# One-hots built by VectorE from broadcast rows of bin numbers, z from full-width operands, two banks for the partial sums

## The reference, cut to what matters

```
msg = silu(concat(h[src], h[dst], weight) @ mW1 + mb1)
msg = layer_norm(msg, ln_g, ln_b)
msg = silu(msg @ mW2 + mb2)
agg = segment_sum(msg, src, num_segments=6250)
```

## Time and profile before

| | |
|---|---|
| median of three runs | 2670.76 us |
| profiled execution, its time / its span | 2670.47 / 2668.8 us |
| sorting ends, first gather of `messages` | 599.5 us, 601.2 us |
| last sum of `messages` ends | 2149.9 us |
| PE / DVE / ACT / POOL busy over the whole span | 76% / 79% / 63% / 66% |
| PE / DVE / ACT / POOL busy from 700 to 1900 us | 1182 / 1119 / 1027 / 967 of 1200 us |
| granted TensorE clock from 700 to 1900 us | 1.00 (2.4 GHz) |
| DMA share and rate from 700 to 1900 us | 0.24, 72 GB/s |

### The profile page before, as it was taken

How to read it: one execution, slowest core, us unless ns; L and a number is a source line. 1 busy time by engine, 2 the same in 40 slices (tenths; PEclk the granted TensorE clock), 3 DMA queues, 4 the chain that set the end, 5 groups by cost and what they waited for, 6 DMA issues and landing times. The chain is left out here.

```text
span 2668.8 us, 63199 instructions
## 1 busy us (share of the span) xinstructions
PE 2025.3 (76%) x14160; PEld 1864.4 (70%) x14161; DVE 2099.3 (79%) x6765; ACT 1692.5 (63%) x3817; POOL 1770.6 (66%) x2247
## 2 busy tenths in 40 slices
PE   0000595008999999999999999999999969829980
PEld 0000584008999999999999999999999857719980
DVE  9994474028999999999999999999999837736666
ACT  5340121027888888888888888888888735418860
POOL 0007777737887878878878788788788715755660
PEclk9999997558999999999999999999999989959995
DMA  5000243012222222222222222222222354434548
GB/s 162 0 0 9 71 145 94 6 37 75 74 71 71 74 71 71 74 72 71 73 72 71 73 71 73 71 73 73 71 72 73 64 170 130 142 122 136 152 140 288
DMA packets 145565, 230.56 MB, mean 86 GB/s; under 512 B 33241, under 2 KB 101491, under 8 KB 145214
## 3 DMA queue, kind: packets, MB, share of 16 engines
q0 software_dynamic: 60672, 139.93, 18.0%
q1 hardware_dynamic: 75758, 81.69, 10.2%
q10 hardware_dynamic: 9040, 7.85, 0.9%
HBM read 167.41 MB, written 61.73 MB: 86 GB/s over the span
## 5 line engine op out<-in xcount | busy, mean ns | idle before, releaser
L1035 POOL DMA_INDIRECT rows<-b_rows,dst_row x838 | 841.8, 1004 | 229.7 <-issue 146.7
L1162 PE MATMUL ps_z<-w_hi,t_hi 128*128 128x256 f32 x1676 | 547.6, 327 | 0.0
L1163 PE MATMUL ps_z<-w_lo,t_hi 128*128 128x256 f32 x1676 | 468.5, 280 | 0.0
L1149 PE MATMUL ps_agg<-rows,onehot 128*126 128x256 f32 x1676 | 454.2, 393 | 18.8 <-DVE node_rows L1184 16.2
L1164 PE MATMUL ps_z<-w_hi,t_lo 128*128 128x256 f32 x1676 | 468.2, 279 | 0.0
L1068 ACT ACTIVATE rows<-rows,shift,rstd_m 128x256 f32<-128x256 f32 x838 | 452.5, 587 | 0.2 <-DVE shift L1192 0.2
L1184 DVE TENSOR_TENSOR node_rows<-node_rows,ps_agg 126x256 f32 x838 | 345.1, 412 | 105.6 <-issue 90.1
L460 POOL DMA_INDIRECT sorted_edges<-pay,place x245 | 242.7, 991 | 279.0 <-DVE place L802 199.4
L1095 ACT ACTIVATE rows<-rows 128x512 f32<-128x512 f32 x419 | 265.0, 632 | 187.9 <-DVE rows L1240 182.2
L1149 PEld LDWEIGHTS ps_agg<-rows,onehot 128*126 128x126 f32 x1676 | 281.3, 187 | 74.4 <-DVE node_rows L1184 23.1
L1045 POOL TENSOR_TENSOR rstd_m<-mv_m,half_m 128x2 f32<-128x2 f32 x419 | 306.3, 731 | 34.9
(11 more groups left out here) (316 smaller groups left out, 4360.3 us busy)
## 6 DMA issues: line engine op xcount, KB each, us to landing
x_e<-by_expert SPq DMA_DIRECT2D x56, 260.0 KB, 2.8
rows<-b_rows,dst_row POOLq DMA_INDIRECT x838
y_back<-y_rows SPq DMA_DIRECT2D x49, 252.0 KB
b_rows<-b_out SPq DMA_DIRECT2D x50, 126.0 KB
u_rows<-u_out SPq DMA_DIRECT2D x50, 126.0 KB
xh_rows<-xh_out SPq DMA_DIRECT2D x50, 126.0 KB
u_row_up<-u_rows SPq DMA_DIRECT2D x50, 126.0 KB
xh_row_up<-xh_rows SPq DMA_DIRECT2D x50, 126.0 KB
```

The source lines that it names most:

```text
L1035: nc.gpsimd.indirect_dma_start(rows[r][:, i, :], None, dram["b_rows"], bass.IndirectOffsetOnAxis(ap=dst_row[:, r, i:i + 1], axis=0)).then_ ...
L1149: mm = pe.matmul(ps_agg[0:BIN, i * D:(i + 1) * D], onehot[:, q, i, 0:BIN], rows[q][:, i, :], start=True, stop=True)
L1162: pe.matmul(z, t_hi[:, k, i, c, :], w2_hi[:, c, :], start=(c == 0), stop=False)
L1163: pe.matmul(z, t_hi[:, k, i, c, :], w2_lo[:, c, :], start=False, stop=False)
```

## The change

Three things are changed in `messages`, and a piece is added to `nodes_and_sort` that feeds the first:

1. The turned one-hots (bin number on the partition, edge along the free dimension) are no longer made on TensorE and copied by ACT. SP loads the row of bin numbers of four tiles into all 128 partitions (`rows_of`, 256 KB every second group) and the two weight words into partitions 126 and 127 of `onehot_t`; DVE compares the row with each partition's number in one `tensor_scalar`. SP's loads are issued two pairs of groups ahead. The small copy L1205 goes, and so do L1128 and L1082.
2. z is four plain float32 products a group instead of twelve float32r ones; the low half L1224 goes, and a `hold` on the statistics takes over its wait.
3. `ps_agg` becomes two banks in place of one, in the room of `ps_oh`; the sums wait for the group before the last instead of the last.

At the end of `nodes_and_sort`, GpSimd copies three of the four words of each edge apart, block by block through three buffers, and SP writes them to the new table `edge_words`.

```diff
+        def words_apart(b):
+            rows = (u_out, xh_out, b_out)[b % 3][:].rearrange("p i f -> p (i f)")[:, 0:(WORDS - 1) * P]
+            return rows.rearrange("p (w e) -> p w e", w=WORDS - 1)
...
             for b in range(BLOCKS):
-                sp.wait_ge(by_tile_in[b], 16)
+                n = min(P, TILES - b * P)
+                sp.wait_ge(words_ready, b + 1)
+                sp.dma_start(dram["edge_words"][:, b * P:b * P + n, :].rearrange("w t p -> t w p"),
+                             words_apart(b)[0:n]).then_inc(words_out[b % 3], 16)
+            for i in range(3):
+                sp.wait_ge(words_out[i], 16 * len(range(i, BLOCKS, 3)))
...
+            for b in range(BLOCKS):
+                n = min(P, TILES - b * P)
+                pool.wait_ge(by_tile_in[b], 16)
+                if b >= 3:
+                    pool.wait_ge(words_out[b % 3], 16 * (b // 3))
+                nc.gpsimd.tensor_copy(words_apart(b)[0:n],
+                                      by_tile[0:n, b, :].rearrange("t (p w) -> t w p", w=WORDS)[:, 1:, :]
+                                      ).then_inc(words_ready, 1)
...
+            def step(j, r, live):    # SP, in messages; AHEAD = 2
+                n = RING * j + r
+                if r % AHEAD or not live(0):
+                    return
+                q = r % (2 * AHEAD)
+                h, many = q // AHEAD, AHEAD if not isinstance(n, int) else min(AHEAD, GROUPS - n)
+                if live(2 * AHEAD):
+                    hold(sp, onehot_t_ready, n - 2 * AHEAD + many)
+                sp.dma_start(rows_of[:, q:q + many].rearrange("p g i e -> p (g i) e"),
+                             dram["edge_words"][0:1, ds(2 * n, 2 * many), :].broadcast_to([P, 2 * many, P])
+                             ).then_inc(rows_in[h], 16)
+                if live(2 * AHEAD):
+                    hold(sp, a_gathered, n - 2 * AHEAD + many)
+                sp.dma_start(onehot_t[BIN:P, q:q + many].rearrange("p g i e -> p (g i) e").bitcast(F32),
+                             dram["edge_words"][1:WORDS - 1, ds(2 * n, 2 * many), :]).then_inc(weights_in[h], 16)
...
-                    nc.vector.tensor_copy(onehot[:, r, :, BIN:P], tiles[:, :, 2:4]).then_inc(onehot_ready, 1)
+                    q = r % (2 * AHEAD)
+                    dve.wait_ge(rows_in[q // AHEAD], 16 * (2 * j + r // 4 + 1))
+                    if live(2 * AHEAD):
+                        dve.wait_ge(a_gathered, n - 2 * AHEAD + 1)
+                    nc.vector.tensor_scalar(onehot_t[0:BIN, q], rows_of[0:BIN, q], pcol[0:BIN, :], None, ALU.is_equal
+                                            ).then_inc(onehot_t_ready, 1)
...
-                    nc.vector.tensor_tensor(t_lo[:, k].rearrange("p i c e -> p (i c e)"), ps_rt[k][:],
-                                            t_hi[:, k].rearrange("p i c e -> p (i c e)").bitcast(F32),
-                                            ALU.subtract).then_inc(lo_ready, 1)
...
-                    if not live(5):
-                        dve.wait_ge(tile_stats, 2 * g + 2)
+                    hold(dve, tile_stats, 2 * g + 2)
...
-                    if live(6 + 1):
-                        pe.wait_ge(added, 2 * g + 1)
+                    pe.wait_ge(onehot_ready, g + 1)
+                    if live(6 + 2):
+                        pe.wait_ge(added, 2 * g - 1)
...
-                            pe.matmul(z, t_hi[:, k, i, c, :], w2_hi[:, c, :], start=(c == 0), stop=False)
-                            pe.matmul(z, t_hi[:, k, i, c, :], w2_lo[:, c, :], start=False, stop=False)
-                            mm = pe.matmul(z, t_lo[:, k, i, c, :], w2_hi[:, c, :], start=False, stop=(c == KC - 1))
+                            mm = pe.matmul(z, t_rows[:, k, i, c, :], w2[:, c, :], start=(c == 0), stop=(c == KC - 1))
```

More of the change, by code:

```diff
@@ L44 @@
 RING = 8
+AHEAD = RING // 4
 TABLE_P = P
@@ L330, in nodes_and_sort @@
         by_tile_turned = sem("by_tile_turned")
+        words_ready = sem("words_ready")
+        words_out = [sem(f"words_out{i}") for i in range(3)]
         slots_even = sem("slots_even")
@@ L483, in _ @@
                     packed[:, n * PACK:(n + 1) * PACK, :].rearrange("h e w -> h (e w)"), None).then_inc(scattered, 16)
+            for k in range(2):
+                pool.wait_ge(outs_stored[k], 16 * 3 * BINS // 2)
+            for b in range(BLOCKS):
[6 more added lines that the diff above has]
+                                      ).then_inc(words_ready, 1)
         @block.scalar
@@ L981, in messages @@
         onehot_ready = sem("onehot_ready")
-        onehot_turned = sem("onehot_turned")
+        rows_in = [sem(f"rows_in{h}") for h in range(2)]
+        weights_in = [sem(f"weights_in{h}") for h in range(2)]
         onehot_t_ready = sem("onehot_t_ready")
@@ L1017, in _ @@
             sp.wait_ge(table_in, 16)
+            def step(j, r, live):
[13 more added lines that the diff above has]
+                             dram["edge_words"][1:WORDS - 1, ds(2 * n, 2 * many), :]).then_inc(weights_in[h], 16)
+            pipeline(sp, step, 0)
         @block.gpsimd
@@ L1023, in _ @@
             nc.gpsimd.memset(half[:], -0.5).then_inc(start, 1)
-            pool.wait_ge(start, 1)
+            nc.gpsimd.iota(pcol[:], [[0, 1]], base=0, channel_multiplier=1, allow_small_or_imprecise_dtypes=True
+                           ).then_inc(start, 1)
+            pool.wait_ge(start, 2)
             def step(j, r, live):
@@ L1075, in step @@
                                          ).then_inc(msg_ready, 1)
[L1076 to L1083, removed]
                 if live(4):
@@ L1089, in step @@
                         act.wait_ge(z_ready, g - 1)
-                    nc.scalar.activation(t_hi[:, k].rearrange("p i c e -> p (i c e)"), ps_rt[k][:], ACT.Copy
-                                         ).then_inc(hi_ready, 1)
+                    nc.scalar.activation(t_rows[:, k].rearrange("p i c e -> p (i c e)"), ps_rt[k][:], ACT.Copy
+                                         ).then_inc(t_ready, 1)
                 if live(1):
@@ L1116, in step @@
                         pre = ps_pre[k][:, i * D:(i + 1) * D]
-                        pe.matmul(pre, onehot_t[:, k, i, :], a_hi[:, ds(b[i], 1), :].rearrange("p o f -> p (o f)"),
+                        pe.matmul(pre, onehot_t[:, q, i, :], a_hi[:, ds(b[i], 1), :].rearrange("p o f -> p (o f)"),
                                   start=True, stop=False)
-                        mm = pe.matmul(pre, onehot_t[:, k, i, :],
+                        mm = pe.matmul(pre, onehot_t[:, q, i, :],
                                        a_lo[:, ds(b[i], 1), :].rearrange("p o f -> p (o f)"), start=False, stop=True)
                     mm.then_inc(a_gathered, 1)
[L1122 to L1129, removed]
                 if live(4):
@@ L1172, in _ @@
             dve.wait_ge(table_in, 16)
+            dve.wait_ge(start, 2)
             def step(j, r, live):
@@ L1178, in add_sums @@
                 def add_sums(i, d):
-                    g = n - d
+                    g, k = n - d, (r - d) % 2
                     dve.wait_ge(part_ready, g + 1)
```

43 lines of the change are left out of this document (18 added, 25 removed).

## The result

The changed kernel takes 2680.36 us (median of 15 runs, 2675.63 to 2691.40) against 2670.76 (15 runs) for the kernel before on the same chip: ratio 1.0032, 95% interval 1.0022 to 1.0042. The forecast was 2682. The sum came out; its terms did not, and the experiments show which.

What follows compares the result with a forecast made beforehand. The prediction took POOL's own instructions, 3.567 us a group, to bound the loop. From the profiled execution: 2670.5 + 5 (once-only) - 6.3 + 12.6 (collisions) = 2681.8, say 2682 us; range 2650 to 2715, the forecast's own 2676 to 2700.

Steps and rivals of the forecast that it cites:

- POOL paces the kernel before at 3.567 us and keeps its pace: Loop: POOL runs its own instructions end to end at 3.567 us a group; disturbances add 0.080, 33.5 us over 419 groups.
- The prediction's own sign of being wrong: Changed loop: the forecast is wrong if L1042 waits for a releaser, or PE has no idle time while POOL has some.
- Once-only, +5: Outside the steady loop: sort's end +3.2 us (+1 to +8), loop's start +2 (0 to +4), sum +5.
- Collisions, -6.3 + 12.6: POOL meeting DVE in the loop: small collisions go, -6.3 us; in one group of eight POOL waits 0.24 longer, +12.6.
- rival B: Loop: shorter and longer collisions cancel, only the once-only 5 us are left, 2675.5 us; chance 0.25.
- z, +0.28 on PE: z's products on PE: twelve take 1.62 us before, four float32 products (eight passes) 1.90 after; 0.28 more work.
- PE's sum +0.03 and hidden: PE's group in the loop: +0.03 us (-0.15 to +0.35), hidden as long as it stays under POOL's.
- rival D: Loop: PE becomes the bound at 3.66 to 3.78 us against 3.647, +5 to +56 us, 2710 in the middle; chance 0.07.
- The banks, nothing won: Two banks for the sums: PE's 0.03 us idle time before L1149 goes, but PE is not the bound, so no gain.
- DVE's issue, 0.7 a group: Sign in the changed profile: DVE's idle time still in front of L1184 and larger, 0.7 us a group.
- DVE's step of 3.52: DVE's loop step, L1240 to L1240: 3.32 us without idle time becomes 3.52, still fitting under POOL's 3.567.
- SP's loads, nothing: SP's 256 KB load every second group: costed at nothing, issued over two groups ahead and hidden by the ring of four groups.

Runs made afterwards that it cites:

- without epsilon: The kernel before with POOL's addition of epsilon to the variance (L1042) left out: ratio 0.9745, 2607.2 us, 3.486 us a group.

## Why the prediction was right in sum, and where its steps failed

That 2682 met 2680 is in part luck: the once-only costs were 2 us too low, the loop's cost 5 us too high, and the two errors met in the sum. The mechanism that held is the one under the sum: POOL went on at its pace, and what was moved to DVE and PE did not lengthen the group.

- *POOL paces the kernel before at 3.567 us and keeps its pace.* Right: 0.25 us taken from POOL alone brings 2.6% there, and the loop holds 329 groups in 1200 us in both kernels. But in the changed kernel POOL no longer paces alone: the same 0.25 us brings 0.6%. The prediction's own sign of being wrong, PE without idle time while POOL has some, was all but seen: PE idles for 7 of 1200 us.
- *Once-only, +5.* The mis-sized term. Its two parts, +3.2 for the sort's end and +2 for the loop's start, measured +6.8 and +0.6. Of the 3.6 us that the sort's end took more, most lies in the rounds. From the first copy to the end of the last they took 10.15 us (593.52 to 603.67), where two rounds of 0.6 and 2.8 and a last copy make 7.4: a copy took 0.87 us, and the buffer of the first write was free 5.33 us after its issue (599.74 - 594.41), the second's 2.20 (602.82 - 600.62). What held the first write up, no row says. The rest, 0.8, lies behind the last copy, 4.33 us, where 2.8 for the write and the 0.7 that the kernel before takes from its last slots (599.49) to POOL's next instruction make 3.5.
- *Collisions, -6.3 + 12.6.* Here the step failed. By place in the loop's eight groups, leaving out the long pauses named at the end, the slow places have means of 3.73 and 3.74 us before and 3.70, 3.65 and 3.75 after; the eight together grew by 0.02, not by 0.24 at one place less 0.015 at each. The comparison cut to two columns gives 0.007 us a group, 3 us, and the intervals of the two times overlap. POOL's meetings with DVE move from one instruction to the other and largely cancel (in ns: L1086 +20, L1089 -10, each gather -3, POOL's idle time -6 a group). The Trainium skill ("SBUF — State Buffer", section "Who interferes with whom") gives the lock on the shared ports, and the rows agree that the engines hold each other up (194 against 206 ns above); that it lengthens a group by as much as I had, no run here shows. This is rival B's mechanism, with a larger once-only price.
- *z, +0.28 on PE.* +0.32: in steps without a wait the float32r products start 0.118 us apart, 12 x 0.118 = 1.41, and the float32 passes 0.216, 8 x 0.216 = 1.73. My two prices were both too high, by about as much. The 1.62 held 0.19 us of the last pass of the sums: z's first start is recorded 0.03 us behind that pass's and the next 0.306 later, and 0.03 + 0.306 is one pass and one product. The 0.24 held the gap behind the first pass of the sums (0.289 in the middle, before; the others are 0.216). The Trainium skill's four passes for true float32 ("FP8 and Floating Point Precision", section "TensorE Precision Notes") would make it, by estimate, 16 x 0.118 = 1.89; the trace has 1.73, so a float32 product costs 3.7 of the others here, still more than the three that it replaces.
- *PE's sum +0.03 and hidden.* The size failed, the hiding held by little: the middle values of the 26 starts of a step without epsilon, before, add up to 3.41 us, and the changed step takes 3.62, +0.21: z +0.32, L1128 -0.22, the gap before the sums and the last turn +0.12. That puts PE 0.05 above POOL's undisturbed pace and 0.03 below its mean, 3.65. So rival D was right that PE becomes a bound, beside POOL; its price (+5 to +56; the middle of it gives 2706, not 2710) was too high because I started from 3.63 for a PE that needs 3.41.
- *The banks, nothing won.* On the changed kernel, where PE is tight, they save 10 us; the kernel before was not run with two.
- *DVE's issue, 0.7 a group.* 0.48. The 0.23 + 0.2 of my own working had it; the 0.7 among the signs does not follow from them. DVE's step of 3.52 added the 0.2 and left out the 0.77 and the 0.41 of the same list; with them it is 3.16. The comparison took 0.374 for 0.41.
- *SP's loads, nothing.* DMA rose from 72 to 108 GB/s, and the loop did not.

## What to carry to other kernels

A busy share of 98.5% says little of an engine's own need: relieve the engine that sets the pace (here by leaving out one small instruction) and read the next bound, before spending one engine's room on another's. When a change leaves the time where it was, it may still have used up all of the slack: here the next good step, worth 2.6% on the old kernel, is worth 0.7% on the new one, other savings included. A stage that ends on GpSimd can cost more than its copies: here 1.6 us beyond its last write.

## What was not expected of the hardware

- Behind its last copy POOL needed 4.33 and 4.34 us until its first instruction of the next stage, in every kernel in which it copied last, whether or not it had waited for writes before.
- ACT's copy of 128x384, four words apart, took 0.90 us, no less than POOL's 0.87.
- DVE's comparison of 126x2 took 300 ns on average; in half of the groups 228 or less, in four of ten 342 or more, next to 348 (the middle value) for 126x256 in the same loop: much of such an instruction's time in this loop is not its elements.
- In all of these kernels one group in fifty takes about 1.5 us longer on POOL (the longest period between groups 20 and 400 is 4.9 to 5.2 us). They are the same groups everywhere, 56, 106, 156 and so on to 406, whether a group takes 3.47 or 3.73 us: the pause follows the count of groups and not the time. No row names a cause.
